# A Flamingo block on one core: the maximum of the last stage taken through a transpose, its rounding on ScalarE

## The reference

```
def fp4_activation(y):                      # one scale for the whole tensor
    scale = max(abs(y)) / 7 + 1e-8
    return clip(round(y / scale), -7, 7) * scale

x2 = x + tanh(g_xattn) * attention_part(layernorm(x), ctx)
y  = gelu(layernorm(x2) @ W1q.T + b1) @ W2q.T + b2      # ternary weights
out = x2 + tanh(g_ffn) * fp4_activation(y)
```

## Time and profile before

| | us |
|---|---|
| median of three runs | 3315.51 |
| lowest and highest run | 3306.97, 3318.33 |
| the profiled execution | 3314.12 |
| its span, first to last instruction | 3312.3 |
| PE, DVE, ACT, POOL busy in it | 3008.0, 2107.4, 1621.5, 1404.1 |
| mean granted TensorE clock | 0.957 |

### The profile page before, as it was taken

The page is one execution under the profiler, slowest core; times in us unless marked ns, Lnnn a source line. Parts: engine busy times, 40 slices in busy tenths (PEclk is TensorE's granted clock), DMA queues, the critical chain, the costliest instruction groups (busy, mean ns, idle before and its releaser), DMA issues. The chain is left out here.

```text
span 3312.3 us, 52045 instructions
## 1 busy us (share of the span) xinstructions
PE 3008.0 (91%) x15500; PEld 1888.7 (57%) x15500; DVE 2107.4 (64%) x4449; ACT 1621.5 (49%) x3005; POOL 1404.1 (42%) x577
## 2 busy tenths in 40 slices
PE   7999999999699999999999999999993588999991
PEld 6777777877444444444444444444431466777771
DVE  5666666666577777767767777777743774443435
ACT  3343334333166666666666666666663653222222
POOL 0000000000067877877877877877873261000000
PEclk9999999999699999999999999999996699999996
DMA  6677777767946676676676776776635261000005
GB/s 171 150 165 165 162 161 165 169 146 156 185 90 123 129 147 127 125 147 116 136 141 114 145 139 116 145 143 112 144 55 146 80 201 32 0 1 0 0 0 203
DMA packets 377445, 401.97 MB, mean 121 GB/s; under 512 B 48304, under 2 KB 298224, under 8 KB 369016
## 3 DMA queue, kind: packets, MB, share of 16 engines
q1 hardware_dynamic: 363272, 323.61, 41.2%
q0 software_dynamic: 9728, 67.12, 14.9%
q10 hardware_dynamic: 4224, 8.39, 0.7%
HBM read 210.77 MB, written 121.15 MB: 100 GB/s over the span
## 5 line engine op out<-in xcount | busy, mean ns | idle before, releaser
L1011 ACT ACTIVATE at_probs<-at_st 128x512 f32<-128x512 f32 (+1 forms) x1664 | 931.4, 597 | 554.2 <-PE at_st L849 533.9
L1041 DVE TENSOR_REDUCE at_cm<-at_mx 128x1 f32<-128x448 f32 x1536 | 855.8, 617 | 339.8 <-PE at_mx L869 336.6
L802 POOL TENSOR_TENSOR at_added<-at_added,at_probs 128x2048 f32<-128x2048 f32 x192 | 889.2, 4631 | 11.5
L849 PE MATMUL at_st<-at_qst,at_kst 101*128 101x512 f32 (+1 forms) x1664 | 651.2, 431 | 9.2 <-ACT at_probs L1011 5.8
L869 PE MATMUL at_mx<-at_kst,at_qst 97*128 97x448 f32 (+1 forms) x2048 | 621.0, 378 | 33.1 <-DMA at_kst<-stack_rows 24.1
L849 PEld LDWEIGHTS at_st<-at_qst,at_kst 101*128 101x128 f32 (+1 forms) x1664 | 295.2, 186 | 438.9 <-ACT at_probs L1011 308.1
L869 PEld LDWEIGHTS at_mx<-at_kst,at_qst 97*128 97x128 f32 x2048 | 398.7, 195 | 192.8 <-DVE at_cm L1041 117.6
L893 PE MATMUL at_acc<-at_probs,at_vt 128*32 128x512 f32 (+2 forms) x3584 | 477.8, 607 | 3.0 <-ACT at_probs L1011 3.0
L770 POOL MEMSET at_ones<- 128x32 f32 x1 | 0.1, 129 | 826.5 <-POOLq L302 826.5
L802 POOL TENSOR_TENSOR at_added<-at_probs 128x2048 f32<-128x2048 f32 x32 | 146.3, 4571 | 307.3 <-PE at_mx L908 251.6
L1555 ACT ACTIVATE ff_h<-ff_psa,ff_b1c,alpha 128x512 f32<-128x512 f32 x128 | 99.5, 778 | 344.6 <-PE ff_psa L1532 344.6
(11 more groups left out here) (205 smaller groups left out, 4710.5 us busy)
## 6 DMA issues: line engine op xcount, KB each, us to landing
at_kst<-k_high SPq DMA_DIRECT2D x256, 200.0 KB
at_probs<-at_probs POOLq DMA_DIRECT2D x32, 1024.0 KB, 7.0
at_kst<-k_low SPq DMA_DIRECT2D x128, 200.0 KB
pj_xin<-in_ctx_dram SPq DMA_DIRECT2D x96, 256.0 KB, 4.4
k_high<-pj_kh SPq DMA_DIRECT2D x96, 256.0 KB, 3.3
k_low<-pj_kl SPq DMA_DIRECT2D x96, 256.0 KB, 4.9
values<-pj_vs SPq DMA_DIRECT2D x96, 256.0 KB, 4.8
at_vt<-values SPq DMA_DIRECT2D x32, 768.0 KB
```

The costliest lines, as they stand in the source:

```text
L802: pool.tensor_tensor(added[:], so_far, probs[:, SLOT[t]], ALU.add).then_inc(S["add_done"], 1)
L849: pe.matmul(st[0:kn, bank, :], kst[g.j][:, h, t * P:t * P + kn], qst[g.j][:, h, :], start=True, stop=True).then_inc(S["st_done"], 1)
L1011: act.activation(probs[0:kn, SLOT[t], h, :], st[0:kn, (NST * g.j + HG * t + h) % 3, :], ACT.Exp, scale=SCALE).then_inc(S["exp_done"], 1)
L1041: dve.tensor_reduce(dst, mx[:, bank % 4, 0:kn], AX.X, ALU.max, negate=last).then_inc(S["mx_free"], 1)
```

## The change

In the last stage, POOL's reduction over the partitions is taken out. DVE copies each partition's maximum across 128 columns, PE transposes that square with the identity matrix of the weight stages, and DVE takes the maximum along the rows of the result in PSUM. The rounding step moves from DVE to ACT, as an Identity with the reciprocal as scale and a column that holds the constant as bias. The hardware loops of SP, ACT and DVE are written out for all eight blocks. ACT's order becomes: rounding of block t, level of block t-1, store of block t-2. DVE's is clip of block t, then the addition of block t-1.

```diff
-def quantize(nc, x2_d, y_all, y_top, g_ffn, out):
+def quantize(nc, ident, x2_d, y_all, y_top, g_ffn, out):
...
-        gate_in, gate = a.sb("gate_in", [P, 1]), a.sb("gate", [P, 1])
-        c = a.sb("c", [P, 8])
+        gate_in, gate, magic = a.sb("gate_in", [P, 1]), a.sb("gate", [P, 1]), a.sb("magic", [P, 1])
+        c, wide = a.sb("c", [P, 8]), a.sb("wide", [P, P])
+        ps = a.banks("ps", 1)
...
-        mine = lambda t: y_all[:, bass.ds(QT * t.n, QT), :]
+        mine = lambda t: y_all[:, QT * t.n:QT * (t.n + 1), :]
...
-            walk(sp, segs, load)
-
-        @block.gpsimd
-        def _(pool):
-            pool.wait_ge(S["rowmax"], 1)
-            pool.partition_all_reduce(c[:, 1:2], c[:, 0:1], P, RMAX).then_inc(S["allmax"], 1)
+            for n in range(B):
+                load(Tile(segs, 0, n // 2, n % 2))
+
+        @block.tensor
+        def _(pe):
+            pe.wait_ge(S["wide_done"], 1)
+            pe.transpose(ps[:, 0, 0:P], wide[:], ident[:]).then_inc(S["allmax"], 1)
...
-            def step(t):
+            def round_up(t):
+                act.activation(mine(t), mine(t), ACT.Identity, bias=magic[:], scale=c[:, 4:5]).then_inc(S["rounded"], 1)
+
+            def level_of(t):
                 act.wait_ge(S["clipped"], t.n + 1)
                 if not early(t.n):
                     act.wait_ge(S["res_done"], t.n - 1)
                 act.activation(level[t.par][:], mine(t), ACT.Copy, bias=-MAGIC).then_inc(S["level_done"], 1)
+
+            def step(t):
+                round_up(t)
                 if not t.first:
+                    level_of(t.prev())
+                if t.n >= 2:
+                    store(t.prev().prev())
+                if t.last:
+                    level_of(t)
                     store(t.prev())
-                if t.last:
                     store(t)
...
-            walk(act, segs, step)
+            act.wait_ge(S["step"], 3)
+            for n in range(B):
+                step(Tile(segs, 0, n // 2, n % 2))
...
             def clip(t):
-                dve.tensor_scalar(mine(t), mine(t), c[:, 4:5], MAGIC, ALU.mult, ALU.add).then_inc(S["rounded"], 1)
                 dve.wait_ge(S["rounded"], t.n + 1)
...
             dve.reduce_max(c[:, 0:1], y_top[:], AX.X).then_inc(S["rowmax"], 1)
+            dve.memset(magic[:], MAGIC)
+            dve.wait_ge(S["rowmax"], 1)
+            dve.tensor_copy(wide[:], c[:, 0:1].to_broadcast([P, P])).then_inc(S["wide_done"], 1)
             dve.wait_ge(S["allmax"], 1)
+            dve.reduce_max(c[:, 1:2], ps[:, 0, 0:P], AX.X).then_inc(S["rowmax"], 1)
+            dve.wait_ge(S["rowmax"], 2)
...
-            walk(dve, segs, step)
+            for n in range(B):
+                step(Tile(segs, 0, n // 2, n % 2))
```

More of the change, by code:

```diff
@@ L1602, in quantize @@
         res = [a.sb(f"res{p}", [P, QT, D]) for p in range(2)]
-        gate_in, gate = a.sb("gate_in", [P, 1]), a.sb("gate", [P, 1])
-        c = a.sb("c", [P, 8])
+        gate_in, gate, magic = a.sb("gate_in", [P, 1]), a.sb("gate", [P, 1]), a.sb("magic", [P, 1])
+        c, wide = a.sb("c", [P, 8]), a.sb("wide", [P, P])
+        ps = a.banks("ps", 1)
         landed = [a.sem(f"landed{p}") for p in range(2)]
         stored = [a.sem(f"stored{p}") for p in range(2)]
-        names = "gate_in_s gate_done rowmax allmax step rounded clipped level_done res_done".split()
+        names = "gate_in_s gate_done rowmax wide_done allmax step rounded clipped level_done res_done".split()
         S = {n: a.sem(n) for n in names}
@@ L1716, in flamingo_block @@
             feed_forward(nc, t1, t2, alpha, b1, b2, xy, y_top)
-            quantize(nc, x2_d, xy, y_top, g_ffn, out)
+            quantize(nc, ident, x2_d, xy, y_top, g_ffn, out)
 _INS = ["x", "ctx_2048", "_lenS2", "g_xattn", "g_ffn", "L0_xattn_w_q", "L0_xattn_b_q", "L0_xattn_w_k", "L0_xattn_b_k",
```

## The result

| | before | changed |
|---|---|---|
| median of 20 runs, us | 3313.98 | 3300.69 |
| lowest and highest | 3305.3, 3318.33 | 3296.36, 3311.03 |
| ratio, 95% interval | | 0.9966 [0.9959, 0.9973] |
| profiled execution, us | 3314.12 | 3298.09 |
| its span | 3312.3 | 3296.3 |

The ratio is 11.3 us of 3314, with an interval from 8.9 to 13.6. That is 2.7 times the 4.2 us forecast, and the median of the changed kernel, 3300.7, lies 3.8 us under the range. The last row of the table is the puzzle: the stage that was edited gave back 4.4 us. In the two profiles the other 11.6 us were gone before it began.

A forecast was written before the change was run, and what follows sets the result against it. The last stage was taken as bound by a serial start and a transfer-limited loop. Leads of 3.3 us (store 1) and 4.5 (load 2) gave 4.2 us: 3309.9 us profiled, 3311.3 against the median, range 3304.5 to 3317.5.

The forecast's parts named there:

- the frame of the sum: Whole program: the last stage is 62 of 3312.3 us, so only a large part of it could visibly matter.
- Part 1: Last stage's start: maximum through PE instead of POOL takes out 8.03 us; coefficients stand 5.7 us earlier.
- The gate set the start: Last stage's start: the reciprocal waits for the gate's Tanh, ending 3253.34, so coefficients stand at 3253.6 instead of 3259.3.
- the second rule: End of last stage: with transfers served in order at full rate, the end moves with load 2, by 4.5 us.
- the first: End of last stage: if store 1 starts 3.3 us earlier and takes the same 10.0 us, the end moves by 3.3.
- ACT's stores: Last stage's fill: store 0 waits behind rounding 2 and level 1, so starts 2.9 us earlier; store 1 3.3 us earlier.
- The rounding's cost in the fill: Last stage, coefficients to first addition and store 0: rounding on ACT costs 1.2 to 2.8 us more.
- two additions wait for a transfer: Last stage's loop before the change: two additions wait for a transfer, one begins as soon as DVE is free.
- the first rival: Last stage's loop: gaps between transfers close too, 5.6 us, giving 3305.7 us; chance 0.13.
- table load: Rival, last stage: Identity and Copy each load a table, 1.283 us twice; ACT sets the pace, 3320.2 us; chance 0.05.
- addition waiting on ACT: Sign that the prediction is wrong: in the last stage's loop, additions wait for ACT; no size given.
- the coefficients did come earlier: Rival, last stage's start, claimed the opposite: something other than POOL held DVE until 3258.9, giving 3317.5 us; chance 0.04.

The follow-up runs named there:

- e1: Changed kernel plus POOL's old reduction over the partitions, run beside the work into a column nobody reads: 3300.1 us, 0.9988 of the kernel before.
- e7: Changed kernel with level and result in place over y, six load buffers, stores by SP, gate load and Tanh in the feed-forward stage: 3282.2 us, ratio 0.9923.
- e8: As e7, with the rounding back on DVE: 3281.8 us, ratio 0.9925 to the kernel before.
- e2: Kernel before plus one addition of one column on POOL behind its last reduction: 3302.5 us, ratio 0.9983.
- e10: Changed kernel plus POOL's reduction beside the work and, behind it, one addition of one column on POOL: 3294.6 us, ratio 0.9970.

## Why the prediction was wrong, step by step

- **The step that failed** is the frame of the sum, "The whole stage is 62 us of 3312.3, so only a large part of it could make a visible difference", and with it Part 1's "It takes out POOL's path, 3258.86 - 3250.83 = 8.03 us". POOL's path had a second piece, 10.55 us of "issue" ahead of L102 at the other end of the program, 5.4 us of it in front of PE. It stood in the profile of before, in the very form of the 7.56 us that the prediction began with the earlier trace rows, and I had read only the stage that was edited. With 3.8 to 5.6 us for it (the three comparisons above) and 4.4 to 4.9 for the stage, the sum is 8.2 to 10.5 us against a measured 8.9 to 13.6, with 11.3 in its middle; so up to some 3 us are not accounted for.
- **The stage itself** came out as predicted: 57.3 us from the end of the row maximum were forecast, and it is 57.06 (3296.3 - 3239.24). The gate set the start, and the coefficients stood 2.8 us behind the row maximum, 3 forecast. The Identity took 2.09 us, 2.1 forecast. Addition 0 ended 11.1 us behind the row maximum's end, 11.3 forecast. That the end fits so well is in part luck. The 4.2 us were chosen between 3.3, from store 1, and 4.5, from load 2. Store 1 was issued 5.7 us earlier and not 3.3 (at 3254.18, which is 14.9 us behind the row maximum's end, 20.7 before), but from its issue to the end the loop took 42.1 us and not 40.8. Load 2, free at the end of addition 0, had its lead of 4.6 us, and the end moved by 4.4: the second rule held, the first did not.
- **ACT's stores** were wrong inside it. "ACT holds rounding 2 (to 3261.8) and level 1 (to 3263.7) ahead of store 0, which waits behind both" did not happen. The store went out at 3250.39, at once with the end of addition 0 and while level 1 was running (3249.87 to 3251.77), and the next activation followed without a gap. So stores 0 and 1 were not late, and ACT's 4.5 us a block were 3.8 (roundings begin at 3247.88 and 3251.67, with store 0 issued between). An issue costs ACT nothing while an activation is running. Where ACT stands idle it does: store 2 is issued at 3261.96 and the rounding behind it begins at 3262.47.
- **The rounding's cost in the fill**, 1.2 to 2.8 us, was 1.0, a little under its lower bound; the upper one came from the late store 0, which was not late.
- **One reading** of the rows was short, though nothing in the sum hangs on it: "two additions wait for a transfer". The earlier trace rows has one such row, and in the whole loop before five of the eight additions wait for a transfer.
- **The gaps** stayed (348 GB/s for 350), as the forecast had it against the first rival. That the buffers cause them is shown by the in-place run.
- **The other rivals** fell: no table load among the last stage's activations, no addition waiting on ACT once the transfers bind the changed kernel's loop (one did in e1, for 2.19 us, and its stage was no longer), and the coefficients did come earlier. The rules of the Trainium skill weighed there fared differently: GPSIMD Engine Reference, Engine selection (the reduction along partitions to GPSIMD) would have kept the dearer path, and ScalarE: Activation LUTs, Rules for kernel authors (multiply and add on VectorE) is right by 1.0 us of the fill in this kernel.
- **Left open.** The middle of the program, the same in all thirteen but for the gate's load and Tanh in e7 and e8, took between 3222.9 and 3238.8 us from the first transpose to the row maximum. The profile of before had the longest. So the 11.6 us by which the two profiles differ at the row maximum hold some 6 us that the start does not explain. Single executions of one kernel lie 13 to 15 us apart, so it may be scatter; no run looked for the cause.

## What to carry to other kernels

When an edit removes an engine's special instruction, look for every idle stretch of that engine that has "issue" as its releaser, over the whole program and at its very start, not in the edited stage alone. Where a program is executed again and again, its end is part of its next start: let POOL end with the library that the next start needs, if need be by a small instruction that nobody waits for. And where each block waits for the store of two blocks before, writing the result in place and giving the space to loads was worth 10 us of the stage (56.1 to 45.8 on one chip; 7.2 us by the medians of the same two), where the transpose, which shortens the chain in front of it, was worth 6.8 (61.7 to 54.9).

## What the runs showed that was not expected

- POOL's change of library, if that is what it is, costs 7.1 to 8.2 us of idle time in the last stage (7.56 before and 8.22 with the rounding alone; 7.33 and 7.06 on the way back, in e2 and e10) and 10.3 to 11.0 at the start of the program, behind a configuration instruction of 11 ns (83 ns on the way back). In the middle of the changed kernel it is there too: configuration at 2599.9, the first tensor on tensor of L1144 at 2608.3. Where the library is already there, the same instruction costs nothing visible (0.50 us from the end of the memset to the affine select). The Trainium skill, GPSIMD Engine Reference, Instruction dispatch, has about 6 us for it; these rows are longer. What is loaded is not seen in a trace; that the cost depends on what POOL did last is. That it carries over to the next execution was seen where the same program is executed repeatedly; its first execution behind another program was not looked at.
- A DMA issue behind an activation in ACT's program goes out while that activation still runs (3250.39 inside 3249.87 to 3251.77): store 0 was not late by the activation ahead of it.
- Two activations of 2.08 and 1.89 us take 3.78 us a pair: each begins about 0.1 us before the last has ended.
